# One transformer layer on one core: the calls on all five engines in a new order, with four waits more

## What is computed

```python
x = x + xattn(ctx, layernorm(x), Wq, Wk, gamma_raw)
x = x + ffn(layernorm(x), w_gate, w_up, w_down)

def xattn(h, adj, Wq, Wk, gamma_raw):
    Q, K = heads(h @ Wq.T), heads(h @ Wk.T)
    sim = einsum('bhnd,bhmd->bnm', Q, K) / (sqrt(d) * H)
    k = int(n * 0.3)
    threshold = top_k(sim, k)[0][:, :, -1:]
    A = sigmoid(sim) * (sim >= threshold)
    A = (A + swapaxes(A, -1, -2)) * 0.5
    gamma = sigmoid(gamma_raw)
    return (1.0 - gamma) * adj + gamma * A

def bitlinear(x, w):        # act_quant: 8 bits a row, weight_quant: -1, 0, 1
    return einsum('bsi,oi->bso', act_quant(rmsnorm(x)), weight_quant(w))

def ffn(x, w_gate, w_up, w_down):
    return bitlinear(silu(bitlinear(x, w_gate)) * bitlinear(x, w_up), w_down)
```

## Time and profile before

| | |
|---|---|
| time, median of 3 runs | 267.66 us (267.48 to 267.7) |
| profiled execution, span from first to last instruction | 265.7 us |
| its own time with what lies around the span | taken as the median; 1.96 us outside the span |
| busy: PE, DVE, ACT, POOL | 81%, 75%, 73%, 62% of the span |
| mean granted TensorE clock | 0.923 of full |
| first `gate` starts on PE | 73.51 us |
| `up(7)` starts on PE | 115.79 us |
| `up(31)`, the last, starts on PE | 250.11 us |

### The profile page before, as it was taken

How to read it: one execution, slowest core, us unless ns; L and a number is a source line. 1 busy time by engine, 2 the same in 40 slices (tenths; PEclk the granted TensorE clock), 3 DMA queues, 4 the chain that set the end, 5 groups by cost and what they waited for, 6 DMA issues and landing times.

```text
span 265.7 us, 3691 instructions
## 1 busy us (share of the span) xinstructions
PE 215.4 (81%) x974; PEld 106.0 (40%) x974; DVE 200.2 (75%) x349; ACT 194.5 (73%) x333; POOL 164.0 (62%) x322
## 2 busy tenths in 40 slices
PE   7704610225898877999999999999999999999995
...
PEclk9985685575799999999999999999999999999999
...
GB/s 129 393 375 360 363 228 401 237 334 202 183 114 86 82 176 153 89 56 1 156 65 0 80 67 84 50 134 146 1 120 31 110 79 46 213 41 78 105 117 214
DMA packets 79143, 39.19 MB, mean 148 GB/s; under 512 B 67984, under 2 KB 70544, under 8 KB 78608
## 3 DMA queue, kind: packets, MB, share of 16 engines
...
## 4 chain that ended last, share of the span: by engine, by line
PE 48%; ACT 18%; DMA 6%; DVE 6%; issue 6%; POOLq 6%; POOL 4%; SPq 2%; DVEq 2%; ACTq 0%
PE DN L424 16%; PE U L405 15%; PE G L391 14%; ACT junk_c L514 6%; DMA C<-in_ctx 5%; ACT WuT L556 2%; ACT sg L539 2%; ACT S L563 2%; POOLq L971 2%; ACT rows L496 1%; SPq L247 1%; POOL qx L1001 1%; DVE m L630 1%; DMA S<-S 1%; ACT junk_h L547 1%
## 5 line engine op out<-in xcount | busy, mean ns | idle before, releaser
L539 ACT ACTIVATE sg<-G,gsc 128x1024 f32<-128x1024 f32 x32 | 35.6, 1113 | 39.5 <-PE G L391 36.2
L391 PE MATMUL G<-WgT,xqT 128*128 128x512 f16 x256 | 60.5, 379 | 4.1 <-ACT sg L539 2.9
L405 PE MATMUL U<-WuT,xqT 128*128 128x512 f16 x256 | 60.5, 379 | 1.7 <-DVE S L759 1.7
L514 ACT ACTIVATE junk_c<-rows,srch 128x512 int8<-128x512 f32 (+1 forms) x76 | 53.9, 719 | 0.9 <-POOL srch L946 0.7
L759 DVE TENSOR_TENSOR S<-U,sg 128x1024 f32<-128x1024 f32 x31 | 37.9, 1223 | 21.3 <-PE U L405 12.8
L424 PE MATMUL DN<-WdT,S 128*128 128x512 f16 x208 | 47.5, 379 | 0.4 <-DMA S<-S 0.4
L1032 POOL TENSOR_SCALAR S<-S,qh 128x2048 f16<-128x2048 f32 x15 | 29.6, 1973 | 26.4 <-DVE qh L822 26.2
L391 PEld LDWEIGHTS G<-WgT,xqT 128*128 128x128 f16 x256 | 24.7, 98 | 35.3 <-ACT sg L539 3.0
L405 PEld LDWEIGHTS U<-WuT,xqT 128*128 128x128 f16 x256 | 24.8, 98 | 32.7 <-DVE S L759 3.9
L547 ACT ACTIVATE junk_h<-S 128x2048 int8<-128x2048 f32 x16 | 30.5, 1907 | 9.0 <-DVE S L774 8.6
L764 DVE TENSOR_REDUCE amh<-S 128x1 f32<-128x2048 f32 x15 | 34.1, 2271 | 0.1
...
## 6 DMA issues: line engine op xcount, KB each, us to landing
...
S<-S SPq DMA_TRANSPOSE x17, 4.3
```

Source lines behind the costliest of these rows:

```text
L391: last = nc.tensor.matmul(G[:, c * 512:(c + 1) * 512], xqT[:, t, k, :], WgT[:, 4 * n:4 * n + 4, k, :], start=(k == 0), stop=(k == KD - 1))
L405: last = nc.tensor.matmul(U[:, c * 512:(c + 1) * 512], xqT[:, t, k, :], WuT[:, 4 * n:4 * n + 4, k, :], start=(k == 0), stop=(k == KD - 1))
L514: A(junk_c[:, j, :].bitcast(U8) if r == ROUNDS else junk_c[:, j, :], ROWS[a % 2][:, j, :], ACT.Sign, bias=nthr[:, j:j + 1], accum_out=cs[: ...
L539: A(sg[:, u % 2, :], G[:, :], ACT.Silu, scale=gsc[:, b % 2, t:t + 1]).then_inc(silu_done, 1)
```

## The change

All five lists of calls are written anew. Every call of before is there once, with the same arguments; so no operation is added or removed. Where an order within the old lists had kept a buffer safe, four waits now stand:

```diff
+        lnc_ready = sem("lnc_ready")
...
             def pre(a):
                 if a in (1, 2):
                     pe.wait_ge(s_ctx2[a - 1], 16)
+                if a:
+                    pe.wait_ge(GT_ready, a)
...
             def sim_stats(a, *js):
                 for j in js:
                     dve.wait_ge(sim_ready, NT * a + j + 1)
                     V.bn_stats(bns[:, j, :], ROWS[a % 2][:, j, 0:N // 2])
+                if a:
+                    dve.wait_ge(thr_act, 2 * rounds_to(a - 1) + js[0] // 2 + 1)
...
             def x_stats(a, *js):
                 if js[0] == 0:
                     dve.wait_ge(s_xin[a], 16)
+                    if a:
+                        dve.wait_ge(lnc_ready, a)
...
             def x1(a, *js):
                     dve.wait_ge(aT_psum, NT * a + j + 1)
+                    if a and j == 0:
+                        dve.wait_ge(xcoef, a)
+                        dve.wait_ge(qx_ready, NT * a)
...
             def ln_coef(a):
-                G_.tensor_tensor(lnc[:, 2, :], lnc[:, 3, :], mvx[:, :, 0], ALU.mult)
+                G_.tensor_tensor(lnc[:, 2, :], lnc[:, 3, :], mvx[:, :, 0], ALU.mult).then_inc(lnc_ready, 1)
...
-            w_load(0, w_gate, 0); w_load(0, w_gate, 1); w_load(0, w_gate, 2); w_load(0, w_gate, 3)
-            w_load(1, w_up, 0); c_load(0, 1, 2); c_load(1, 2, 4); x_load(0); w_load(1, w_up, 1)
+            w_load(0, w_gate, 1); w_load(0, w_gate, 0); c_load(0, 1, 2); w_load(0, w_gate, 2); w_load(0, w_gate, 3)
+            x_load(0); w_load(1, w_up, 0); w_load(1, w_up, 3); w_load(1, w_up, 2); w_load(1, w_up, 1); x_load(3)
...
-            evac_hT(0); evac_GT(0); sims(0, 0); sims(0, 1); sims(0, 2); sims(0, 3); w_abs(0, 1); counts(0, 0, 0)
+            evac_hT(0); evac_GT(0); w_abs(0, 1); sims(0, 0); sims(0, 1); tanhs(0, 0); sims(0, 2); sims(0, 3)
```

More of the change, by code:

```diff
@@ L873, in _ @@
-            x_stats(1, 2, 3); x1(0, 0); x1(0, 1); w_quant(1, 0); x1(0, 2); x1(0, 3); x_absmax(0, 0); x_scale(0, 0)
-            x_absmax(0, 1); x_scale(0, 1); w_quant(1, 1); x_absmax(0, 2); x_scale(0, 2); x_absmax(0, 3)
-            x_scale(0, 3); rank(1, 0); rank(1, 1); rank(1, 2); rank(1, 3); w_quant(1, 2); w_quant(1, 3)
-            note_misses(1); threshold(1); general_path(1); masked(1, 0); masked(1, 1); masked(1, 2); w_scale(2)
-            masked(1, 3); mul(0); sim_stats(2, 0, 1); x1(1, 0); w_quant(2, 0); mul(1); sim_stats(2, 2, 3)
@@ L893, in _ @@
[L893 to L895 removed]
+            w_abs(0, 0); sim_stats(0, 0, 1); sim_stats(0, 2, 3); w_abs(0, 2); w_abs(0, 3); x_stats(0, 0, 1)
```

188 lines of the change are left out of this document (95 added, 93 removed).

## The result

The median is 276.72 us (274.21 to 280.08) against 267.68 (267.48 to 267.74): the ratio is 1.0307, with a 95% interval of 1.0287 to 1.0327. The ratios leave out the profiled executions, and this one also the longest, 280.08, so they are not the quotients of the medians. The kernel became 3.1% slower; the forecast was 264.5, 1.2% faster. The profiled execution of after took 275.97, with a span of 274.2, so 1.8 us lie outside the span (1.96 before).

A forecast was written before the change was run, and what follows sets the result against it. ACT, with DVE close behind, was taken to bound the first 117 us, PE 115.79 to 250.11, then a tail. Terms -5.4 + 1.9 + 0.3 = -3.2 gave span 262.5, time 264.5, range 260.3 to 269.0.

The forecast's parts named there:

- Durations cancel and only positions count.: Whole kernel: every operation is kept, so its duration stays as before and only its place in the order matters.
- the ramp: From `silu(0)` to `up(7)`: where the change earns its time, `up(7)` at 110.4 against 115.79, a gain of 5.4 us.
- solid part: From `up(7)` to `up(31)`, PE's work: new waits of 2.8 us together, 1.9 more than before.
- Front: Up to `silu(0)`, counted by ACT's calls ahead of it: `silu(0)` at 75.7, a gain of 1 us.
- (a): ACT from `silu(0)` to the eighth `silu`: 9.2 us less work in a stretch that held 40.62 without idle time.
- (b): DVE: `mul(0)` at 77.0, 5.6 us earlier, `mul(6)` between 104.6 and 107.2, `up(7)` by 108.4 at the latest.
- (c): SP's queue: w_down transposes wait for `w_quant(2,0)` at about 93, land at about 107, and put `up(7)` at 110.4.
- rival 4: PE before `up(7)`: one to three units at the lower clock cost 1.7 to 5.2 us; 266.2 to 269.7, chance 0.05.
- Tail: From `up(31)` to the end: five stores instead of four wait behind the last transposes, 0.3 us more.
- the four waits: New waits in `pre`, `sim_stats`, `x1` and `x_stats`, the only thing added; all priced at 0.
- rival 3: Element 2 comes late: `x_coef(2)` ends at 176.6, `gate(17)` starts 4.8 us later; time 269.3, chance 0.16.
- Rival 2: Gain given back: PE comes 5.4 us earlier into attention work of elements 2 and 3, and waits; 267.6, chance 0.11.

The follow-up runs named there:

- the hold: The new order, but POOL's first `add_a` of elements 0 and 3 waits for all four `masked` on DVE; 271.44 us, ratio 1.0180.
- the last kernel: The new order with calls moved to mend the late places its traces named, and POOL's added wait before `add_a` taken out again; 266.25 us, ratio 0.9957.

## Why the prediction was wrong

**"Durations cancel and only positions count."** This is the step that failed. The prediction took every duration from a row of before and moved it to a new place. Four `masked` and a `w_quant` then took 8.6 us where the rows gave 4.7, since the new place is beside POOL's `add_a`; two `masked` beside `h_round(0)` took 3.12 instead of 1.40 and cost PE 1.52 in the ramp; the four of element 3 (4.75) cost PE 1.90 in the solid part. The hold, on elements 0 and 3, gave 3.4 to 5.5 us back, less than half of the 12.2 between forecast and result. As far as the traces show, the rest lies in queues that the prediction didn't walk, named below: with them mended as well the kernel came to 266.2, within 1.7 of the forecast, but what each move gave stays open. The Trainium skill, SBUF — State Buffer, section "SBUF: two separate sides", says that VectorE and GpSimd share a pair of ports, locked for a whole instruction by whichever starts first, if the VectorE operation has a 2-port fast mode, or two inputs in SBUF while the GpSimd operation reads SBUF. The rows agree on which operations meet: `masked` has two such inputs, and `x1`, whose one input is in PSUM (TR), kept its 0.68 beside the `add_a` of 54.10 with the hold. They don't show that one blocks the other for its whole length: four `masked`, a `w_quant` and four `add_a` are 9.8 us alone and were through in 8.6, though POOL's times are rough.

**Front.** Counting ACT's calls needs ACT to be without idle time in the new order too; it stood 4.70 us before `centre(0, 0)`. Of the 5.4 by which `silu(0)` is late, the hold gave 1.7 back. The 2.58 that `rank(0, 0)` waited for thresholds behind `ln_coef(0)` on POOL is a queue that the prediction didn't walk. Even with both gone, `silu(0)` is at 78.39, 1.7 later than before and 2.7 later than forecast: it waits 0.82 there for `x_coef(0)` on POOL, which the prediction had named, and ACT has 1.7 us of shorter waits from `centre(0, 0)` on. The rest I did not take apart.

**Ramp, (a) and (b).** The count of what leaves ACT held: from `silu(0)` to the eighth `silu` ACT works 31.88 us, forecast 40.62 - 9.2 = 31.4. In after nothing of the gain was left: `up(1)` waited for transposes of w_up, and `a_transposes(1, 0)` and `up(5)` for DVE, which took 34.1 us from `mul(0)` to `mul(6)` (83.31 to 117.45) where (b) allowed 30.2. With these places mended, `silu(0)` to `up(7)` takes 112.75 - 78.39 = 34.4 us, forecast 34.7, before 39.1.

**Ramp, (c).** `w_quant(2, 0)` was forecast for 93 and started at 101.67: 5.4 of the 8.7 came in with `silu(0)`, the rest arose between the two. The prediction named this as what comes last; it did, by 0.39. But the same queue held `up(1)` as well, for 2.39, where SP's new order puts `xq(0, 1)`, `xq(0, 2)` and a load ahead of four transposes of w_up. They took 7.93 to issue, 5.37 before. The prediction looked at SP for `down(0)` alone.

**The clock**, rival 4, had 0.05 and a price of 1.7 to 5.2. It took part: in after once (`up(1)`, 1.4), in the kernel with `ln_coef` moved twice (3.1). The Trainium skill, TensorE: Matmul & The Clock Gate, part 1, says that an idle array falls back to 1.2 GHz. The rows of after agree: `up(1)` runs at a granted clock of 0.56 behind 2.39 us of waiting. By the rows of before, which showed no such fall in the ramp, I gave the rival little. The error was to take the absence of long waits for granted, when the change itself brought them.

**Solid part.** +1.9 forecast, +3.15 in after, of which 1.90 is `a_transposes(3, 0)`. Without that wait it was +1.94 with the hold and +1.56 in the last kernel. That these sizes are near the forecast's is luck, since the places were others: `sims(3, 1)`, `down(6)` and `up(23)` did not wait in after; `up(13)` (1.39, for `mul(12)`) did.

**Tail.** 0.3 forecast, 1.2 measured: a term that was mis-sized. It counted issues only. From the end of the last half `final` to the end of the span it was 2.2 before and 3.4 after, because the last half store goes out with the stores that had been put off (204 GB/s in that stretch, 152 before). With three stores moved forward it was 2.1, and the stretch 15.5.

**Right**: the price of 0 for the four waits, though `ln_coef(1)` ended at 71 and not by 64, and `x_stats(2)` waited 1.18 for it; and rival 3 not taken as the forecast: `gate(17)` started at 181.69 directly behind `down(6)`, without a wait.

**Rival 2** had the sign of giving back, but not the mechanism: the gain went to transposes and to DVE in the ramp, not to attention work behind it.

Open: why the runs of after differ among themselves by more than those of before (274.2 to 277.5 without the longest). Only one of them has a trace. That the clock at `up(1)` and `down(0)` falls in some and not in others would be enough for it; the mean granted clock of the two longer (0.899 and 0.901, against 0.912 and 0.913) fits that, but doesn't show it, since the executions of before reach from 0.903 to 0.923 at one time. Nor was it separated which of the moves in the last kernel are needed.

One reading was loose: PE's tenths are solid from the seventeenth slice on and not the twentieth, and the clock's already from the twelfth. Nothing in the sum hangs on it.
